# The last step of a four-layer gated graph network: work of the final half-graph dealt out again among VectorE, GpSimd and ScalarE

## What is computed

```python
h = x
for i in range(L):
    hw = jnp.einsum('bnc,cd->bnd', h, weight[i])
    m = jnp.einsum('bjn,bjd->bnd', adj, hw)
    h = _gru_cell(m, h, w_ih[i], w_hh[i], b_ih[i], b_hh[i])
# _gru_cell:
#   r = sigmoid(xr + hr); z = sigmoid(xz + hz); n = tanh(xn + r * hn)
#   return (1.0 - z) * n + z * h
y = x + h * mask[:, :, None]
out = (y - mean(y)) / sqrt(var(y) + 1e-5)      # over the 128 channels
```

## Time and profile before

| | us |
|---|---|
| median of three runs | 542.04 (541.89 to 542.56) |
| the profiled execution, its own time | 542.58 |
| the profiled execution, its span | 540.5 |
| PE, busy in the span | 514.6 (95%) |
| DVE / ACT / POOL, busy in the span | 385.6 / 381.0 / 218.7 |

### The profile page before, as it was taken

One profiled execution on the slowest core, in us unless ns is written; L12 is line 12 of the kernel. 1 busy time (PEld: TensorE's weight loads), 2 busy tenths in 40 slices (PEclk: granted clock), 3 DMA queues, 4 the chain that ended last, 5 costly groups with the idle time before them and its releaser, 6 DMA issues.

```text
span 540.5 us, 7419 instructions
## 1 busy us (share of the span) xinstructions
PE 514.6 (95%) x2288; PEld 422.3 (78%) x2288; DVE 385.6 (71%) x688; ACT 381.0 (70%) x628; POOL 218.7 (40%) x161
## 2 busy tenths in 40 slices
PE   5899999999999999999999999999999999999960
PEld 4688888888888888888888888888888888888740
DVE  3687567675788886666688886666778886676666
ACT  4577777648776788857786788874886778884422
POOL 2044332443345454443236554333254644334432
PEclk9999999999999999999999999999999999999985
DMA  8941554265732456274662165364473166433302
GB/s 295 384 180 59 173 210 163 74 179 155 257 116 78 128 191 208 90 222 130 188 238 85 58 212 215 97 205 144 138 271 98 59 213 215 136 113 111 109 19 81
DMA packets 78911, 85.12 MB, mean 157 GB/s; under 512 B 3784, under 2 KB 61728, under 8 KB 78880
## 3 DMA queue, kind: packets, MB, share of 16 engines
q1 hardware_dynamic: 78608, 84.60, 47.0%
q10 hardware_dynamic: 272, 0.13, 0.1%
HBM read 64.27 MB, written 20.45 MB: 157 GB/s over the span
## 4 chain that ended last, share of the span: by engine, by line
PE 89%; DVE 3%; DMA 2%; SPq 1%; issue 1%; POOL 1%; ACT 1%; DVEq 0%; ACTq 0%; POOLq 0%
PE p_S L478 39%; PE p_r L488 5%; PE p_r L492 5%; PE p_r L489 5%; PE p_z L488 5%; PE p_z L492 5%; PE p_z L489 5%; PE p_hn L488 3%; PE p_hn L492 3%; PE p_hn L489 3%; PE p_xn L492 3%; PE p_xn L488 3%; PE p_xn L489 3%; DMA adj_in<-in_adj_dram 1%; PE p_tr L426 1%
## 5 line engine op out<-in xcount | busy, mean ns | idle before, releaser
L1235 POOL TENSOR_TENSOR work<-hT,work 128x512 f32<-128x512 f32 x63 | 87.8, 1394 | 268.5 <-ACT work L684 268.5
L478 PE MATMUL p_S<-adj_hi,nat_hi 128*128 128x512 f32 x480 | 187.4, 391 | 0.0
L478 PE MATMUL p_S<-adj_hi,nat_lo 128*128 128x512 f32 x480 | 186.8, 389 | 0.0
L478 PEld LDWEIGHTS p_S<-adj_hi,nat_hi 128*128 128x128 f32 x480 | 90.1, 188 | 18.9 <-DVE nat_lo L855 0.3
L478 PEld LDWEIGHTS p_S<-adj_hi,nat_lo 128*128 128x128 f32 x480 | 90.1, 188 | 18.5
L1107 DVE SCALAR_TENSOR_TENSOR work<-p_hn,bias,work 128x512 f32<-128x512 f32 x62 | 46.5, 749 | 76.5 <-ACT work L684 76.3
L1239 POOL TENSOR_TENSOR work<-work 128x512 f32<-128x512 f32 x63 | 90.1, 1430 | 4.9
L684 ACT ACTIVATE work<-p_r,bsum 128x512 f32<-128x512 f32 x63 | 43.3, 687 | 56.3 <-PE p_r L492 56.1
L891 DVE STREAM_TRANSPOSE work<-hT 128x512 f32<-128x512 f32 x62 | 69.1, 1115 | 2.1
L684 ACT ACTIVATE work<-work,bias 128x512 f32<-128x512 f32 x63 | 45.7, 726 | 34.1 <-DVE work L1111 28.6
L656 ACT ACTIVATE low_words<-adj_in 128x1024 bf16<-128x1024 uint16 x64 | 67.1, 1048 | 1.0
(11 more groups left out here) (137 smaller groups left out, 918.5 us busy)
## 6 DMA issues: line engine op xcount, KB each, us to landing
adj_in<-in_adj_dram SPq DMA_DIRECT2D x72, 512.0 KB, 6.7
bounce<-work SPq DMA_DIRECT2D x62, 256.0 KB, 2.0
low<-bounce SPq DMA_DIRECT2D x62, 256.0 KB, 2.8
x_in<-in_x_dram SPq DMA_DIRECT2D x8, 512.0 KB, 7.1
y<-in_x_dram SPq DMA_DIRECT2D x8, 512.0 KB, 4.3
out_dram<-y SPq DMA_DIRECT2D x7, 512.0 KB, 4.2
y<-in_L_gnn_w_ih_dram SPq DMA_DIRECT2D x2, 192.0 KB, 7.2
y<-in_L_gnn_w_hh_dram SPq DMA_DIRECT2D x2, 192.0 KB, 8.0
```

What stands on the lines that cost most here:

```text
L478: last = nc.tensor.matmul(p_S[h][:, :], part[:, s, j], adj_hi[:, s, j, half(h)], start=(j == 0 and part is nat_hi), stop=(j == NB - 1 and ...
L1235: nc.gpsimd.tensor_tensor(t_sb[:, h], hT[:, s, half(h)], n_sb[:, h], ALU.subtract).then_inc(d_sub, 1)
```

## The change

All of it lies in the last step and behind it.

- **DVE.** `gated` and `candidate` of graph 7's half 0 come ahead of graph 6's residual. Graph 6's second residual comes ahead of half 1's `S_lo`. The add of half 0's state (L950) and its residual (L994) leave DVE. `make_shift` of graph 6 moves behind 1-z. Behind the new state of half 1 its two quarters are added and measured, and rows 4 to 7 share one set of moments; then rows 0 to 3 are measured, and only rows 2 and 3 are normed by DVE.
- **POOL.** It adds half 0's state, and behind z*h it adds the masked half 0 to `y` (128x512). It takes two powers of four columns in place of three.
- **ACT.** It masks half 0's transposed blocks from PSUM into `n_sb`, two ahead of half 1's sigmoids and two behind them. All eight norm blocks of graph 6 come after the tanh of half 1, then rows 4 to 7 and then rows 0 and 1 of graph 7.
- **SP.** Two stores of 256 KB, rows 4 to 7 and then rows 0 to 3, in place of three on two queues.

```diff
 # ScalarE
+            def mask_turned(blocks):
+                act.wait_ge(h_tr, 1)
+                for j in blocks:
+                    last = nc.scalar.activation(n_sb[:, 0, j * C:(j + 1) * C], p_tr[0][:, j, :], ACT.Copy,
+                                                scale=mask[:, (B - 1) * NB + j:(B - 1) * NB + j + 1])
+                if blocks.stop == HB:
+                    last.then_inc(tr_masked, 1)
...
-                act.wait_ge(shift_made, B - 1)
-                normalise_former(range(0, NB // 4))
+                mask_turned(range(0, HB // 2))
...
                 gate(z_sb[:, 1], p_z[:, :], z_done, z_act, ACT.Sigmoid, b_z, p, k)
+                mask_turned(range(HB // 2, HB))
...
-            normalise_former(range(NB // 4, NB))
-            store_last(act, 1)
+            act.wait_ge(shift_made, B - 1)
+            scale_blocks(0, range(NB)).then_inc(y0_normed, 1)
+            act.wait_ge(last_shift, 1)
+            scale_blocks(1, range(HB, NB)).then_inc(last_normed, 1)
+            act.wait_ge(last_shift, 2)
+            scale_blocks(1, range(0, HB // 2)).then_inc(last_normed, 1)
 # VectorE
+            def last_moments(rows, made):
+                for j in range(rows.start, rows.stop):
+                    last = nc.vector.bn_aggr(mv[:, 1, j], stats[:, j])
+                last.then_inc(last_aggr, 1)
+                dve.wait_ge(last_aggr, made)
+                nc.vector.tensor_scalar(vare[:, 1, rows], mv[:, 1, rows, 1], EPS, None, ALU.add).then_inc(last_var, 1)
+            def make_last_shift(rows, made):
+                dve.wait_ge(last_rstd, made)
+                nc.vector.scalar_tensor_tensor(shift[:, 1, rows], mv[:, 1, rows, 0], -1.0, rstd[:, 1, rows], ALU.mult,
+                                               ALU.mult).then_inc(last_shift, 1)
...
+                for n in range(2):
+                    last_residual(p, n)
+                    last_measure(p, n)
+                dve.wait_ge(last_stats, 2)
+                last_moments(LAST_ROWS, 1)
+                dve.wait_ge(last_added, 1)
+                for j in range(HB):
+                    last = nc.vector.bn_stats(stats[:, j], y[:, 1, j])
+                last.then_inc(last_stats, 1)
+                make_last_shift(LAST_ROWS, 1)
+                dve.wait_ge(last_stats, 3)
+                last_moments(FORMER_ROWS, 2)
+                make_last_shift(FORMER_ROWS, 2)
+                for j in range(HB // 2, HB):
+                    last = nc.vector.tensor_scalar(y[:, 1, j], y[:, 1, j], mv[:, 1, j, 0:1], rstd[:, 1, j:j + 1],
+                                                   ALU.subtract, ALU.mult)
+                last.then_inc(middle_normed, 1)
 # GpSimd
+                        if last and g == STEPS - 1:
+                            pool.wait_ge(d_mul, HS * p + k + 1)
+                            nc.gpsimd.tensor_tensor(hT[:, s, half(h)], n_sb[:, h], t_sb[:, h],
+                                                    ALU.add).then_inc(h_new, 1)
...
+            pool.wait_ge(tr_masked, 1)
+            pool.wait_ge(y_loaded[1], 16 * PAIRS)
+            nc.gpsimd.tensor_tensor(y[:, 1, FORMER_ROWS], y[:, 1, FORMER_ROWS],
+                                    n_sb[:, 0].rearrange("p (j c) -> p j c", c=C), ALU.add).then_inc(last_added, 1)
```

More of the change, by code:

```diff
@@ L187, in gnn_kernel @@
         n_kept = sem("n_kept")
+        tr_masked = sem("tr_masked")
+        last_added = sem("last_added")
+        last_stats = sem("last_stats")
+        last_aggr = sem("last_aggr")
+        last_var = sem("last_var")
+        last_rstd = sem("last_rstd")
+        last_shift = sem("last_shift")
+        last_normed = sem("last_normed")
+        middle_normed = sem("middle_normed")
         h_kept = sem("h_kept")
@@ L971, in candidate @@
                 nc.vector.tensor_tensor(t_sb[:, h, cols], p_xn[:, cols], t_sb[:, h, cols], ALU.add).then_inc(t_add, 1)
-            def last_normalise(n):
-                dve.wait_ge(rstd_made, B + n)
-                for j in range(LAST_BLOCKS[n].start, LAST_BLOCKS[n].stop):
-                    last = nc.vector.tensor_scalar(y[:, 1, j], y[:, 1, j], mv[:, 1, j, 0:1], rstd[:, 1, j:j + 1],
-                                                   ALU.subtract, ALU.mult)
-                last.then_inc(y_normed, 1)
-            def last_variance(p, n):
-                blocks = LAST_BLOCKS[n]
-                dve.wait_ge(y_stats, 4 * p + 2 + n + 1)
-                for j in range(blocks.start, blocks.stop):
-                    last = nc.vector.bn_aggr(mv[:, 1, j], stats[:, j])
-                last.then_inc(y_aggr, 1)
-                dve.wait_ge(y_aggr, 2 * p + 1 + n + 1)
-                nc.vector.tensor_scalar(vare[:, 1, blocks], mv[:, 1, blocks, 1], EPS, None, ALU.add).then_inc(var_eps, 1)
-            def last_half_residual(p):
-                dve.wait_ge(y_loaded[1], 16 * (p + 1))
-                dve.wait_ge(h_tr, 1)
-                for j in range(HB):
-                    last = nc.vector.scalar_tensor_tensor(y[:, 1, j], p_tr[0][:, j, :], mask[:, (B - 1) * NB + j:(B - 1) * NB + j + 1],
-                                                          y[:, 1, j], ALU.mult, ALU.add)
-                last.then_inc(y_added, 1)
             def last_residual(p, n):
@@ L1008, in last_measure @@
             def last_measure(p, n):
-                dve.wait_ge(y_added, 4 * p + 3 + n + 1)
-                for j in range(LAST_BLOCKS[1 + n].start, LAST_BLOCKS[1 + n].stop):
+                dve.wait_ge(y_added, 4 * p + 2 + n + 1)
+                for j in range(HB + n * (HB // 2), HB + (n + 1) * (HB // 2)):
                     last = nc.vector.bn_stats(stats[:, j], y[:, 1, j])
-                last.then_inc(y_stats, 1)
+                last.then_inc(last_stats, 1)
[9 more added lines that the diff above has]
+                                               ALU.mult).then_inc(last_shift, 1)
             def last_step(p):
@@ L1020, in last_step @@
                 turn(p, g - 1, 1)
+                gated(p, k, 0, whole)
+                candidate(p, k, 0, whole)
                 residual(p, 0, 0)
                 measure(p, 0, 0)
-                gated(p, k, 0, whole)
-                candidate(p, k, 0, whole)
                 wait_stats(p, 0, 0)
                 moments(0, 0)
+                residual(p, 0, 1)
                 s_low(p, g, 1)
-                new_state(p, g, 0)
-                residual(p, 0, 1)
                 measure(p, 0, 1)
@@ L1044, in last_step @@
                 nc.vector.tensor_scalar(r_sb[:, 1], z_sb[:, 1], -1.0, 1.0, ALU.mult, ALU.add).then_inc(z_rest, 1)
-                measure(p, 1, 0)
+                make_shift(p, 0)
                 dve.wait_ge(z_rest, 1)
@@ L1253, in _ @@
                                         ALU.mult).then_inc(h_kept, 1)
-            for n, blocks in enumerate(LAST_BLOCKS):
-                pool.wait_ge(var_eps, B + n)
-                nc.gpsimd.tensor_tensor(rstd[:, 1, blocks], vare[:, 1, blocks],
-                                        mhalf[:, 0:blocks.stop - blocks.start], ALU.pow).then_inc(rstd_made, 1)
+            pool.wait_ge(tr_masked, 1)
+            pool.wait_ge(y_loaded[1], 16 * PAIRS)
+            nc.gpsimd.tensor_tensor(y[:, 1, FORMER_ROWS], y[:, 1, FORMER_ROWS],
+                                    n_sb[:, 0].rearrange("p (j c) -> p j c", c=C), ALU.add).then_inc(last_added, 1)
+            for n, rows in enumerate((LAST_ROWS, FORMER_ROWS)):
+                pool.wait_ge(last_var, n + 1)
+                nc.gpsimd.tensor_tensor(rstd[:, 1, rows], vare[:, 1, rows], mhalf[:, 0:HB],
+                                        ALU.pow).then_inc(last_rstd, 1)
             def graph(b):
```

37 lines of the change are left out of this document (12 added, 25 removed).

## The result

| | before | after |
|---|---|---|
| median of five runs, us | 542.03 (541.88 to 542.56) | 539.48 (538.82 to 539.85) |
| the profiled execution, its own time | 542.58 | 538.82 |
| the profiled execution, its span | 540.5 | 537.0 |

The ratio of the times is 0.9947, with a 95% interval of 0.9936 to 0.9958: 2.6 us less, where 2.1 less (539.9) was forecast. The two spans differ by 3.5 us, more than the medians. Both kernels are alike up to the last step, but its first 512-column sigmoid stands at 511.43 before and at 511.13 after, and in the other profiles of this study between 510.45 and 513.02, in kernels that hold the same instructions up to there.

What follows compares the result with a forecast made beforehand. PE bounds up to half 0's last product of the last step, then a chain over all engines with three queue-order delays. Terms -5.6, +1.75, +1.65 and +0.1 give -2.1, from 542.04 to 539.9 us; range 537.3 to 541.0.

Steps and rivals of the forecast that it cites:

- Half 0 and r: Last step: half 0's gates taken earlier, and ACT's r of half 1 at 520.5 instead of 526.10, 5.6 us earlier.
- POOL's chain: Power, z*h and add to `y` ahead of half 1's new state, with DVE held, give back 1.75 us.
- rival (1): No holding: DVE and POOL pass each other, new state at 523.9, 2.5 us less, 537.4; chance 0.10.
- The tail: From the new state to the last store: two powers in series and ACT's blocks give back 1.65 us.
- The stores: Behind the last issue: same trickling end as before, plus 0.1 us for a last store of 256 KB.
- rival (3): The slow trickle of data behind the last store is gone, 538.4 us; chance 0.09.
- The sum: All terms of the last step and end together: -2.1 us, from 542.04 to 539.9; chance 0.50.
- rival (5): Slower: half 1's load of `low` lands late, delaying DVE's queue; gain gone from 3 us, 543.1 at 4; chance 0.04.

Runs made afterwards that it cites:

- e1: The changed kernel, but POOL's add of the masked half 0 to `y` waits until half 1's new state is finished; 537.64 us, ratio 0.9909.
- e2: The changed kernel with graph 6's second residual put back behind half 1's `S_lo` on DVE; 539.36 us, ratio 0.9944.
- e3: The changed kernel with half 0's state added by DVE again, ahead of graph 6's second residual, not by POOL; 538.99 us, ratio 0.9939.
- e4: The kernel before with one edit: DVE takes half 0's `gated` and `candidate` ahead of graph 6's first residual and moments; 539.72 us, ratio 0.9949.
- e6: e4 with ACT's wait for graph 6's shift and all its norm blocks behind half 1's tanh; 539.09 us, ratio 0.994.
- e1_again: The kernel of e1 run again in a later set on another chip; 538.88 us, ratio 0.9943.
- e5: e1 with graph 6's power behind z*h on POOL and its shift behind the new state on DVE; 538.71 us, ratio 0.9933.
- e9: e5 with one more wait: POOL's add of the masked half 0 also waits for graph 6's shift; 537.97 us, ratio 0.9921.
- e7: e6 with DVE's shift of graph 6 and half 0's residual behind 1-z; 538.68 us, ratio 0.9925.
- e8: Against e5, POOL's add to `y` in its idle time ahead of z*h, with masks, measures, powers, norms and stores rearranged; 536.45 us, ratio 0.9894.

## Why the prediction was right, point by point

**Half 0 and r (-5.6).** Measured -5.48 from the anchor (14.67 to 9.19). POOL's add of the state took 1.28 (1.3 forecast), PE's wait 0.39 (0.4), the residual ended 0.68 behind POOL (0.67). PE's wait for `S_lo` was 0.15 instead of 0.4; r is at 520.32, which is 520.6 on before's clock. (The forecast wrote 518.65 for the state where its own terms, 517.25 and 1.3, give 518.55; it was 518.69 on that clock.)

**POOL's chain (+1.75).** The sequence came as forecast: power 521.14 (521.15), z*h 522.76 to 524.43, the add to `y` from 524.38 to 525.82 (to 525.75), the new state behind it, its quarter ending 3.94 earlier than before where 3.84 was forecast for its start. One detail was wrong. I let two DVE operations pass and had the second product wait out the add. The shift, the first and the second product all passed at POOL's boundaries, or behind them (the pair of products 1.28 long), and the state's first quarter waited itself, for 1482 ns. The end came out nearly the same, since either way something waits for POOL's add, and a part of that is luck: a second product that waited out the add would have stood ahead of the state with the rest of its own work, which the forecast's 526.1 leaves out. e1 takes the add away and gets 1.1 back, so rival (1), no holding, is excluded, and e1 is what it would have looked like in part.

**The tail (+1.65).** Measured +1.3, and most of the difference is luck. The forecast took the way from the new state to the first add from before, where PE's first pair of transposes took 0.69. After, it took 0.44, and the second pair 0.48 instead of 0.63. The granted clock shows why. Busy time by stretch (columns as in the earlier trace rows), three stretches of after, and the transposes of before:

```profile
518.36:520.85 2.49, 2.25 (x11) 1.64 (x12) 2.46 (x12) 1.16 (x4) 0.03 (x1) 1.00 0.00 0
522.10:524.69 2.59, 0.00 (x0) 0.00 (x0) 2.52 (x7) 2.17 (x6) 2.59 (x4) 1.00 0.00 0
526.17:527.00 0.83, 0.81 (x4) 0.40 (x4) 0.63 (x3) 0.56 (x2) 0.00 (x0) 0.86 0.00 0
...
530.40:531.52 1.12, 1.11 (x4) 0.67 (x4) 1.09 (x8) 0.71 (x2) 0.26 (x1) 0.50 0.00 0
```

The clock was at its upper level, 2.4 GHz, through the products, as the prediction had taken. It stayed there from 522.10 to 524.69 with PE idle, where before had 0.51, and was 0.86 in the stretch of the last transposes, ahead of which PE had stood 4.57 us. The prediction carried the upper level to the products only, and charged the transposes at the lower one. In e2 and e3, which have the same tail, the transposes did run at the lower one, and the stretch from state to issue is 7.24 and 7.23: +1.6, as forecast. The other 0.1 is the pitch of the rounds of add and measure, 527.69 - 526.64 = 1.05 instead of 1.17. It isn't the clock's, as DVE did not wait for PE there: the second add starts 0.40 behind the start of the measure (527.29 to 527.69), and the forecast had put 0.52 there, at which `bn_aggr` followed the measure in before.

**The stores (+0.1).** This step failed, by 0.65: the stretch from the last issue to the end went from 4.13 to 3.58. DMA by slices of 0.09 us, first the mean busy share and then GB/s, of after from 533.4 on:

```profile
DMA  8999899996031030048999999995100000000000
GB/s 262 296 284 267 262 273 273 296 256 148 17 108 17 17 114 23 17 125 262 307 279 307 296 290 279 284 296 154 51 23 0 0 0 0 0 0 0 0 0 0
```

and the GB/s of before, whose busy shares are in the earlier trace rows:

```profile
GB/s 302 273 262 307 324 279 262 256 279 302 284 279 444 262 273 376 239 234 120 29 6 11 11 17 17 23 23 11 11 11 23 17 23 23 23 0 0 0 0 0
```

Before, the bulk was through after 19 slices, and 16 slices, 1.4 us, of 6 to 29 GB/s followed. After, such a trickle (mostly 17 to 23 GB/s) lies between the two stores, and two slices follow the last one. Both profiles have fetches of instructions among the transfers. That the fetch moves with the stores was not tested; what the runs show is that the trickle is not a fixed part of an order of stores: e4 and e6 end with the same three stores, and have 4.16 and 3.44. So the 0.55 belongs to rival (3) in part. The table says a little more: the seven profiles with the two stores of the change (after, e1 to e3, e1_again, e5, e9) end 3.32 to 3.72 behind the last issue, the four with before's three stores 3.44 to 4.28. Three of these four lie above all seven. A shorter end thus goes with the change in most executions, but what makes it is not shown.

**The sum.** From the anchor -5.48 + 1.54 + 1.33 - 0.55 = -3.16; the medians say -2.55. The profiled execution of after (538.82) is the fastest of its five, and that of before (542.58) lies above all of its five, so the profiles overstate the gain. Against the forecast's -2.1, the anchored sum is off by +0.1 at r, -0.2 in POOL's chain, -0.3 in the tail and -0.65 at the stores; the tail's and a part of the stores' are of the execution that was profiled.

**What the prediction did not ask.** It rated the edits as one. e4 and e7 show that they are unequal: by the last issue, the gates first, -2.5; both orders of the shift, -1.6 more; POOL's part with the residual's new place and ACT's masks, +0.2; the new tail, +1.3. The sum had +1.75 and +1.65 as the cost of moves and never asked what before's tail would give behind the new orders. e7 is that kernel, and it is ahead. `low`, rival (5), was 0.38 us late for DVE after its measure and by the timeline it cost nothing: the residual's first block, started at 516.22, was held to the end of POOL's product at 517.04.

**A rule against a row.** In e5 DVE's two quarters of the new state, both inputs in SBUF, ran from 523.28 to 524.02 at their unheld 0.74, within POOL's power of 522.70 to 524.52. So POOL's 8-column power did not hold DVE, while its 256- and 512-column operations did in the lists above. e9 (524.42 to 525.17 within a power of 523.84 to 525.66) and e8 show the same. The Trainium skill (SBUF — State Buffer, "Who interferes with whom") has the lock between two such operations kept for the whole instruction. For the wide operations the traces agree (1.82 us after against 0.75 in e1); for the narrow power the measurement decides, and it was free.

## What to carry to other kernels

First look for an operation that stands in a queue behind work that nobody waits for: moving two lines gave as much here as the whole rewrite, and a wait moved on one engine paid only when its twin on the next engine moved too. Work given to POOL was cheap only where POOL was idle and DVE not at operations with two inputs in SBUF; a hold of 1.1 us went away by starting POOL's add later or, better, in an idle gap before. To compare edits in a tail of 30 us out of 540, measure from a common instruction just ahead of them, since the front scatters by more than the edits are worth; and look at the granted clock at short TensorE work behind an idle stretch before a difference of 0.2 us is put down to an edit.

## What was unexpected of the hardware

- A hold lasts as long as POOL's instruction and a little more: a 256-column add on DVE that waited ended 0.3 us behind it. Of graph 6's four residual blocks one waited out the add, and it and the two behind it were through 0.68 us after the add. POOL itself grew little: z*h from 1.59 to 1.67 for its two quarters, the add from 1.27 (e1, alone) to 1.44.
- A narrow operation on DVE is held as well: the shift of 8 columns, 0.17 us alone, took 1.22 beside POOL's 512-column add (e5, e9).
- POOL's power of 8 columns took 1.64 to 1.82 us and of 4 columns 1.01 to 1.03, and DVE's adds ran unheld beside the first (e5, e8, e9).
- The span ended 3.44 or 4.16 us behind the last issue of the same three stores (e6, e4).
- The first pair of half 1's transposes took 0.44 us at a granted clock of 1.00 and 0.61 at 0.62, in two executions of one kernel with the same 3.50 us of idle PE ahead (e1_again, e1).
